# Gathering expert rows two tiles ahead, and a new order at the start of the expert stage

## The chip, the cores and the metric

The kernel runs on one core of one Trainium2 chip. The metric is the device time of one execution in microseconds (us). A time given for a kernel is the median of several executions; rows and durations come from one profiled execution.

The engines are named as the profile names them: PE (TensorE, matrix products; PEld is its weight load), ACT (ScalarE), DVE (VectorE), POOL (GpSimd), SP (SyncE, which here only issues DMAs).

## The reference

One transformer layer over `x` of 32 x 64 tokens of 256 numbers, all float32: a routed mixture of 8 experts, an attention block, a second attention block with a coherence gate, and an FFN with 4-bit rounding. The change touches the expert stage only:

```
gate   = rms_norm(x) @ wg_W + wg_b + cond @ gg_W + gg_b
topk_w, topk_i = top_k(softmax(gate), 2)            # two experts for each token
h1 = relu(x  @ W1[e] + b1[e])                       # 256 -> 512
h2 = relu(h1 @ W2[e] + b2[e])                       # 512 -> 512
out_e = h2 @ W3[e] + b3[e]                          # 512 -> 256
out = sum over the two chosen experts of topk_w * out_e
```

The kernel computes, for each token, only the two experts that were chosen.

## The kernel before

**Tiles.** The 2048 tokens times two choices are sorted by expert into `SLOT_TILES` = 36 tiles of 128 rows. Tiles 0 to 7 hold the first block of expert 0 to 7 each; tiles 13 to 15 are "mixed" (two experts, 64 rows each); the others belong to one expert that is looked up at run time. For each tile the rows of `x` are fetched by an indirect DMA (a *gather*), turned by PE so that features lie on partitions, and sent through three layers.

**Engines in the expert stage.** Every engine has its own program in a fixed order; semaphores join them. A step `j` on PE is `expert_step(j)` (lines 833 to 845): layer 1 of tile `j+1`, the turn of tile `j+2` (`turn_x`, L745, two transposes), layer 2 of tile `j`, layer 3 of tile `j-1`. The loop starts at `j = -2`, so the first steps are short: the turn of tile 0; then layer 1 of tile 0 and the turn of tile 1; then layer 1 of tile 1, the turn of tile 2 and layer 2 of tile 0.

- POOL issues the gathers (L612) into four buffers `xg0` to `xg3`, in tile order, and between them the gathers of bias rows for the mixed tiles (L623 for `b1`, L630 for `b2`).
- ACT copies a turned tile from PSUM into the one buffer `xg_t` (`copy_x`, L1378) and applies bias and rectifier after layer 1 (`relu1`, L1395, four activations of 128 x 128). `relu1` first reads the expert's number into a register (L1389, a TENSOR_LOAD and two register instructions).
- DVE copies the expert's first and second weight matrix into `w1_now` (L1910) and `w2_now` (L1926), and does the second rectifier (L1951).
- SP loads the experts' weights into `arena`, each expert in two halves of 1024 KB (L543). At most two halves are under way: a half is issued when the same half of the expert before has landed. From expert 3 on the load overwrites the scratch of the routing, so the first half of expert 3 also waits for `arena_free` and for the first two gathers (lines 537 to 541).

Layer 1 of tile `j` on PE waits for three things: `xt_set` (the copy of that tile), `h1t_set` (the rectifier of the tile before, which frees the PSUM bank), and `w1_set` (the weights). The turn of tile `j` waits for its gather and for the copy of the tile before.

**Before the first turn** PE runs `keep_busy(40)` (L735, L676): 40 products of 128 x 128 in bfloat16 whose result nobody reads.

The parts of the program that the change touches, with the line numbers of the profile:

Of the kernel before, what the change touches and what calls it, by code (L numbers as in the profile page):

```python
# [54 lines left out]
SLOT_TILES = FULL + MIXED  # L55
# [15 lines left out]
FI = 0.3 * 0.7  # L71
RMS_EPS, LN_EPS, MOD_EPS = 1e-6, 1e-5, 1e-8
XG = 4
TINY, FP4_MAX = 1e-30, 6.0
ROUND = 1.5 * 2.0 ** 22
NEG = -3.0e38
# [25 lines left out]
def exists(t, n):  # L102

    return not isinstance(t, int) or 0 <= t < n
# [17 lines left out]
def mixed(p):  # L122

    return FIRST_MIXED <= p <= LAST_MIXED


def nth(p):

    return p - FIRST_MIXED if mixed(p) else p if p < FIRST_MIXED else p - MIXED


def slot_tile(p):


    if p < EXP:
        return p
    if p < FIRST_MIXED:
        return HOST + p - EXP
    return FULL + nth(p) if mixed(p) else nth(p) - (FULL - HOST)
# [26 lines left out]
def build(nc, t_in, out):  # L166
    ctx = ExitStack()
    with ctx:
# [37 lines left out]

        xg = [sb(f"xg{n}", [P, HID]) for n in range(XG)]
        xg_t = sb("xg_t", [P, KH, P])
# [215 lines left out]
        field_loaded = sem("field_loaded")  # L424
        x_gathered = [sem(f"x_gathered{n}") for n in range(XG)]
        xt_ps = sem("xt_ps")
# [91 lines left out]
        @block.sync  # L518
        def _(sp):

            sp.dma_start(cols[:, 0:GATE_COLS], t_in["cols"][:, 0:GATE_COLS]).then_inc(cols_loaded, 16)
            for k in range(KH):
                sp.dma_start(x_t[:, k, :], t_in["x_t"][k * P:(k + 1) * P, :]).then_inc(xt_loaded[k], 16)
            for k in range(KH):
                sp.wait_ge(xt_loaded[k], 16)
            sp.dma_start(cols[:, GATE_COLS:col_n], t_in["cols"][:, GATE_COLS:col_n]).then_inc(small_loaded, 16)
            sp.dma_start(rows[:, :], t_in["rows"].to_broadcast([P, row_n])).then_inc(small_loaded, 16)
            sp.dma_start(we2, t_in["we2_t"].rearrange("(k p) n -> p k n", p=P)).then_inc(small_loaded, 16)
            sp.dma_start(w_delta, t_in["ffn_dw"].rearrange("(k p) n -> p k n", p=P)).then_inc(small_loaded, 16)
            sp.dma_start(setup_rows, t_in["setup_rows"].to_broadcast([P, set_n])).then_inc(small_loaded, 16)  # L530


            for e in range(EXP):
                for n in range(2):
                    if e:
                        sp.wait_ge(moe_loaded[n], 16 * e)
                    if e == SETUP_FROM and n == 0:

                        sp.wait_ge(arena_free, 1)
                        for g in range(2):  # L540
                            sp.wait_ge(x_gathered[g], 16)
                    at = n * E_SIZE // 2
                    sp.dma_start(arena[:, e * E_SIZE + at:e * E_SIZE + at + E_SIZE // 2],  # L543
                                 t_in["experts"][e][:, at:at + E_SIZE // 2]).then_inc(moe_loaded[n], 16)
                if e == SETUP_FROM - 1:
                    sp.dma_start(b3[:, :], t_in["b3"].to_broadcast([P, EXP * HID])).then_inc(b3_loaded, 16)
                if e == SETUP_FROM + 1:
                    sp.dma_start(w_raw, t_in["ffn_w"].rearrange("(k p) n -> p k n", p=P)).then_inc(ffn_loaded, 16)
            for half in range(2):
                sp.dma_start(half_rows[half * SEQ:(half + 1) * SEQ, :],  # L550
                             t_in["half_rows"][half:half + 1, :].to_broadcast([SEQ, half_n])).then_inc(half_loaded, 16)
            sp.wait_ge(setup_done, 1)
            sp.wait_ge(fa_stored, 16)
            sp.wait_ge(y_ps, LAST_MIXED + 1)
            for dst, name in ((wq, "wq"), (wk, "wk"), (wv, "wv"), (wo, "wo")):
                sp.dma_start(dst[:, :, :], t_in[name].rearrange("(k p) n -> p k n", p=P)).then_inc(w1_loaded, 16)


            sp.wait_ge(w1_set, SLOT_TILES)
            for dst, name in ((wq2, "wq2"), (wk2, "wk2"), (wv2, "wv2"), (wc1, "wc1"), (wout2, "wout2")):  # L560
                sp.dma_start(dst, t_in[name].rearrange("(k p) n -> p k n", p=P)).then_inc(l2w_loaded, 16)
            sp.dma_start(x_in, t_in["x"][0:P, :]).then_inc(x_tile, 16)
            sp.wait_ge(w2_set, SLOT_TILES)
            sp.dma_start(field_t.rearrange("p t q -> p (t q)"),
                         fa_out.rearrange("(o b) q -> o (b q)", o=1).to_broadcast([P, BATCH * SEQ])).then_inc(field_loaded, 16)
            for t in range(TT + 2):
                if exists(t - 2, TT):
                    sp.wait_ge(fin_set, t - 1)
                    sp.dma_start(out[(t - 2) * P:(t - 1) * P, :], fin[t % 2]).then_inc(stored[t % 2], 16)
                if exists(t + 1, TT):  # L570
                    sp.wait_ge(x1_set, t + 1)
                    sp.dma_start(x_in, t_in["x"][(t + 1) * P:(t + 2) * P, :]).then_inc(x_tile, 16)
            for n in range(2):
                sp.wait_ge(stored[n], 16 * TT // 2)
# [3 lines left out]
        def _(pool):  # L578
# [28 lines left out]


            for j in range(SLOT_TILES):
                if j >= XG:  # L610
                    pool.wait_ge(xt_ps, j - XG + 1)
                pool.indirect_dma_start(  # L612
                    out=xg[j % XG][:, :], out_offset=None, in_=t_in["x"],
                    in_offset=bass.IndirectOffsetOnAxis(ap=slot_tok[:, slot_tile(j):slot_tile(j) + 1], axis=0)).then_inc(x_gathered[j % XG], 16)
                if mixed(j - 2):
                    n = nth(j - 2)
                    if n == 0:
                        pool.wait_ge(row_expert_set, 1)
                        pool.wait_ge(setup_done, 1)
                        pool.wait_ge(fa_stored, 16)  # L620
                    if n >= BIAS_BUFS:
                        pool.wait_ge(h1r_set, n - BIAS_BUFS + 1)
                    pool.indirect_dma_start(  # L623
                        out=b1_rows[n % BIAS_BUFS], out_offset=None, in_=t_in["b1"],
                        in_offset=bass.IndirectOffsetOnAxis(ap=row_expert[:, n:n + 1], axis=0)).then_inc(b1_gathered[n % BIAS_BUFS], 16)
                if mixed(j - 4):
                    n = nth(j - 4)
                    if n >= BIAS_BUFS:
                        pool.wait_ge(h2r_set, n - BIAS_BUFS + 1)
                    pool.indirect_dma_start(  # L630
                        out=b2_rows[n % BIAS_BUFS], out_offset=None, in_=t_in["b2"],
                        in_offset=bass.IndirectOffsetOnAxis(ap=row_expert[:, n:n + 1], axis=0)).then_inc(b2_gathered[n % BIAS_BUFS], 16)
# [36 lines left out]
        def _(pe):  # L669
# [3 lines left out]
            def keep_busy(n):  # L673

                for _ in range(n):
                    mm(bank(6, P), ones[:, :], ones[:, :], start=True, stop=True)  # L676
# [55 lines left out]
            for k in range(KH):  # L732
                last = mm(ps[0:BATCH, 7, 0:HID], f_hid[:, k, :], we2[:, k, :], start=k == 0, stop=k == KH - 1)
            last.then_inc(fp_ps, 1)
            keep_busy(40)  # L735

            pe.wait_ge(experts_set, 1)
            flat = arena[:, :]
# [603 lines left out]
        def _(act):  # L1342
# [31 lines left out]
            def copy_x(j):  # L1374
                act.wait_ge(xt_ps, j + 1)
                if j:
                    act.wait_ge(l1_ps, j)
                act.copy(xg_t[:, :, :], ps[:, 5, 0:KH * P].rearrange("p (k q) -> p k q", k=KH)).then_inc(xt_set, 1)  # L1378
# [48 lines left out]
            def expert_step(j):  # L1427
                if mixed(j - 1):
                    take_w3(j - 1)
                    if exists(j + 2, SLOT_TILES):  # L1430
                        copy_x(j + 2)
                    relu2_mixed(j - 1)
                    store_y(j - 2)
                    if exists(j + 1, SLOT_TILES):
                        relu1(j + 1)
                else:
                    if exists(j + 1, SLOT_TILES) and not mixed(j + 1):
                        relu1(j + 1)
                    if exists(j + 2, SLOT_TILES):
                        copy_x(j + 2)  # L1440
                    if j == 0:
                        relu2_first()
                    if mixed(j + 1):
                        relu1(j + 1)
                if exists(j - 1, SLOT_TILES) and not mixed(j):
                    store_y(j - 1)
# [12 lines left out]
            for j in range(-2, LAST - 1):  # L1459
                expert_step(j)  # L1460
                side_stage(j)
# [986 lines left out]
```

## Time and profile before

| | |
|---|---|
| median of 3 runs | 742.73 us (741.77 to 743.66) |
| profiled execution, its own time | 744.68 us |
| its span, first to last instruction | 743.2 us |
| mean granted TensorE clock | 0.986 of full |
| busy: PE, DVE, ACT, POOL | 713.3, 486.3, 287.8, 90.9 us |
| chain that ended last, by engine | PE 94%, DVE 3%, ACT 1%, issue 1% |

The profile lists instructions by start and duration, with the idle time of the engine before them and what ended it. The chain is found by going back from the last instruction, at each step to what released it. Starts are recorded, the ends of products are modelled. The expert stage lies between about 33 and 300 us of the span; the change acts on its first 15 us and on the order of the gathers throughout it.

### The profile page before, as it was taken

The page shows a single profiled execution, that of the slowest core. Times are in us where ns is not written, and L with a number is a line of the kernel's source. Part 1 is how long each engine was busy: PE and PEld are TensorE (multiplying, and loading weights), DVE is VectorE, ACT ScalarE, POOL GpSimd, SP SyncE. Part 2 cuts the span into 40 slices and gives each one's busy share as a digit, 9 for nine tenths or more (in the row PEclk, how much of TensorE's full clock was granted, in tenths as well). Part 3 has the DMA queues.
Part 4 walks back from the last instruction along what each step waited for, and adds up shares of the span by engine and source line. Part 5 has one row for each costly group of instructions (what it writes and reads, how often), then busy time and mean ns, then how long its engine had stood idle before and what let it go on. Part 6 is the DMA issues. An engine that isn't in the chain of part 4 may idle for free.

```text
span 743.2 us, 20463 instructions
## 1 busy us (share of the span) xinstructions
PE 713.3 (96%) x8266; PEld 615.5 (83%) x8266; DVE 486.3 (65%) x1036; ACT 287.8 (39%) x839; POOL 90.9 (12%) x102
## 2 busy tenths in 40 slices
PE   6389999999999999999999999999999999999997
PEld 4279999559999999978778878978888897888785
DVE  4756565743545444334777787787778778777867
ACT  3032121142121221253465446445544654564552
POOL 2121112411111101031101101110110111000000
PEclk9599999999999999999999999999999999999999
DMA  7998111217111102310001000000110010000000
GB/s 262 336 353 322 37 37 56 81 43 257 50 37 37 37 30 69 118 50 23 16 9 30 30 7 25 30 23 10 30 31 9 23 30 24 8 16 16 9 9 23
DMA packets 21402, 49.13 MB, mean 66 GB/s; under 512 B 3323, under 2 KB 14971, under 8 KB 18749
## 3 DMA queue, kind: packets, MB, share of 16 engines
q1 hardware_dynamic: 12256, 32.47, 12.2%
q0 software_dynamic: 3744, 10.49, 4.7%
q10 hardware_dynamic: 5309, 4.87, 2.0%
q8 instruction: 66, 1.08, 0.6%
q14 instruction: 27, 0.22, 0.1%
HBM read 41.00 MB, written 6.82 MB: 64 GB/s over the span
## 4 chain that ended last, share of the span: by engine, by line
PE 94%; DVE 3%; ACT 1%; issue 1%; another core or an unknown queue 0%; DVEq 0%; POOL 0%; ACTq 0%; POOLq 0%
PE ps L897 16%; PE ps L796 15%; PE ps L766 8%; PE ps L923 8%; PE ps L830 7%; PE ps L982 7%; PE ps L948 4%; PE ps L998 3%; PE ps L941 2%; PE ps L973 2%; PE ps L1013 2%; PE ps L1075 2%; PE ps L1032 2%; PE ps L790 1%; PE ps L676 1%; PE ps L1045 1%
## 5 line engine op out<-in xcount | busy, mean ns | idle before, releaser
L897 PE MATMUL ps<-arena,l_weights 128*128 128x128 f32 x1024 | 125.9, 277 | 0.5 <-ACT arena L1470 0.5
L796 PE MATMUL ps<-h_t,w_now 128*128 128x128 f32 x1056 | 123.4, 275 | 1.2 <-DVE h_t L1951 1.2
L796 PEld LDWEIGHTS ps<-h_t,w_now 128*128 128x128 f32 x1056 | 120.5, 192 | 1.4 <-issue 1.4
L897 PEld LDWEIGHTS ps<-arena,l_weights 128*128 128x128 f32 x1024 | 119.3, 192 | 2.3 <-ACT arena L1470 1.0
L1395 ACT ACTIVATE h_t<-ps,cols 128x128 f32<-128x128 f32 x132 | 37.8, 367 | 163.9 <-PE ps L766 149.5
L1926 DVE COPY w_now<-arena 128x2048 f32 x33 | 40.5, 1227 | 83.2 <-PE ps L796 74.7
L1476 ACT ACTIVATE arena<-ps,cols 128x128 f32<-128x128 f32 x256 | 73.9, 387 | 48.0 <-PE ps L897 48.0
L645 POOL DMA_INDIRECT arena<-expert_out,slot_of x32 | 33.1, 1033 | 323.0 <-DVE arena L1979 272.8
L766 PEld LDWEIGHTS ps<-xg_t,w_now 128*128 128x128 f32 x528 | 63.4, 192 | 6.0 <-ACT xg_t L1378 3.5
L766 PE MATMUL ps<-xg_t,w_now 128*128 128x128 f32 x528 | 65.0, 276 | 3.0 <-ACT xg_t L1378 3.0
L612 POOL DMA_INDIRECT xg<-in_x,slot_tok x36 | 41.6, 1155 | 186.4 <-PE ps L745 157.4
L830 PE MATMUL ps<-arena,h_t 128*128 x264 | 62.5, 380 | 0.0
L923 PE MATMUL ps<-l_weights,arena 128*64 128x512 f32 x256 | 61.8, 605 | 0.0
L830 PEld LDWEIGHTS ps<-arena,h_t 128*128 128x128 f32 x264 | 47.7, 191 | 5.1
L982 PE MATMUL ps<-l_weights,arena 128*128 128x256 f32 x224 | 51.5, 383 | 0.0
L982 PEld LDWEIGHTS ps<-l_weights,arena 128*128 128x128 f32 x224 | 41.5, 190 | 5.2
L1910 DVE COPY w_now<-arena 128x1024 f32 x33 | 22.9, 694 | 29.3 <-PE ps L766 20.7
L1951 DVE TENSOR_SCALAR h_t<-ps,cols 128x128 f32<-128x128 f32 x128 | 35.8, 342 | 4.6 <-PE ps L796 4.5
L948 PE MATMUL ps<-ident,arena 128*128 128x128 f32 x256 | 38.3, 273 | 0.1
L2097 DVE TENSOR_TENSOR arena<-ps,half_rows 128x512 f32<-128x512 f32 x32 | 21.9, 686 | 22.7 <-PE ps L973 17.2
L923 PEld LDWEIGHTS ps<-l_weights,arena 128*64 128x64 f32 x256 | 15.6, 136 | 22.5 <-issue 21.4
L1559 ACT ACTIVATE arena<-arena 128x512 f32<-128x512 f32 x32 | 20.2, 631 | 31.6 <-DVE arena L2180 31.6
(366 smaller groups left out, 1097.1 us busy)
## 6 DMA issues: line engine op xcount, KB each, us to landing
arena<-in_experts SPq DMA_DIRECT2D x16, 1024.0 KB
expert_out<-y ACTq DMA_DIRECT2D x36, 128.0 KB
arena<-in_x_t SPq DMA_DIRECT2D x2, 1024.0 KB, 6.2
arena<-in_x SPq DMA_DIRECT2D x16, 128.0 KB
out<-arena SPq DMA_DIRECT2D x16, 128.0 KB, 1.7
b<-in_b SPq DMA_DIRECT2D x1, 1024.0 KB
l_weights<-in_wq SPq DMA_DIRECT2D x1, 1024.0 KB
l_weights<-in_wk SPq DMA_DIRECT2D x1, 1024.0 KB
```

The lines of the kernel that those rows point to most:

```text
L612: pool.indirect_dma_start(out=xg[j % XG][:, :], out_offset=None, in_=t_in["x"], in_offset=bass.IndirectOffsetOnAxis(ap=slot_tok[:, slot_ti ...
L766: last = mm(ps[:, 0, m * P:(m + 1) * P], w1_now[:, k, m * P:(m + 1) * P], xg_t[:, k, :], start=k == 0, stop=k == KH - 1)
L796: last = mm(ps[:, 2, m * P:(m + 1) * P], w2_now[:, k, m * P:(m + 1) * P], h1_t[j % 2][:, k, :], start=k == 0, stop=k == KM - 1)
L830: last = mm(bank(4, HID), h2_t[j % 2][:, k, :], flat[:, bass.ds(at + k * HID, HID)], start=k == 0, stop=k == KM - 1)
L897: last = mm(ps[:, b, c * P:(c + 1) * P], wt[:, k, f:f + P], m_t[:, k, :], start=k == 0, stop=k == KH - 1)
L923: last = mm(ps[r * SEQ:(r + 1) * SEQ, value_bank(t, s), :], m_t[:, k, s * SEQ:(s + 1) * SEQ], wv[:, k, r * 512:(r + 1) * 512], start=k == ...
L948: last = pe.transpose(bank_[:, m * P:(m + 1) * P], p[:, h:h + 2, :], ident[:, :])
L982: last = mm(bank(1, HID), ctx_t[:, c, :], wo[:, c, :], start=c == 0, stop=c == C1 - 1)
L1395: last = f(h1_t[j % 2][:, k, :], ps[:, 0, k * P:(k + 1) * P], ACT.Relu, bias=cols[:, bass.ds(e * KM + at + k, 1)])
L1476: last = f(dst[:, cc, :], ps[:, project_bank(t, n), c * P:(c + 1) * P], ACT.Tanh, bias=col(bias)[:, cc:cc + 1])
L1926: dve.tensor_copy(w2_now[:, :, :].rearrange("p k n -> p (k n)"), arena[:, bass.ds(at, KM * MID)]).then_inc(w2_set, 1)
L1951: last = ts(h2_t[j % 2][:, k, :], ps[:, 2, k * P:(k + 1) * P], cols[:, bass.ds(e * KM + at + k, 1)], 0.0, ALU.add, ALU.max)
```

## The change

Five edits, no change to what is computed:

1. Gather `j` waits until tile `j - 2` is turned (`AHEAD` = 2) where it waited until tile `j - 4` was turned (`XG` = 4 buffers). The four buffers stay. Only two gathers go out at once at the start.
2. The bias gathers keep their place in the stream counted by turned tiles: `b1` of tile `j` follows the gather of tile `j` and not of tile `j + 2`; `b2` likewise.
3. The first half of expert 3 waits for three gathers and not for two.
4. `keep_busy` before the first turn has 28 products and not 40.
5. In ACT's step `j = -1` the copy of tile 1 comes ahead of the rectifiers of tile 0.

```diff
--- before
+++ after
+AHEAD = 2
...
                         sp.wait_ge(arena_free, 1)
-                        for g in range(2):
+                        for g in range(3):
                             sp.wait_ge(x_gathered[g], 16)
...
             for j in range(SLOT_TILES):
-                if j >= XG:
-                    pool.wait_ge(xt_ps, j - XG + 1)
+                if j >= AHEAD:
+                    pool.wait_ge(xt_ps, j - AHEAD + 1)
                 pool.indirect_dma_start(
...
-                if mixed(j - 2):
-                    n = nth(j - 2)
+                if mixed(j):
+                    n = nth(j)
...
-                if mixed(j - 4):
-                    n = nth(j - 4)
+                if mixed(j - 2):
+                    n = nth(j - 2)
...
-            keep_busy(40)
+            keep_busy(28)
...
                 else:
+                    if j == -1:
+                        copy_x(j + 2)
                     if exists(j + 1, SLOT_TILES) and not mixed(j + 1):
                         relu1(j + 1)
-                    if exists(j + 2, SLOT_TILES):
+                    if exists(j + 2, SLOT_TILES) and j != -1:
                         copy_x(j + 2)
```

On ACT, at the start of the expert stage (line, instruction, output<-input; TENSOR_LOAD and the ISA rows read the expert's number), the order before is:

```order
L1378 COPY xg_t<-ps 128x256 [waits xt_ps,experts_set]
L1389 TENSOR_LOAD tile_expert
L1389 ISA x2
L1395 ISA [waits l1_ps]
L1395 ACTIVATE h1_t0<-ps,cols 128x128
L1395 ISA
L1395 ACTIVATE h1_t0<-ps,cols 128x128
L1395 ISA
L1395 ACTIVATE h1_t0<-ps,cols 128x128
L1395 ISA
L1395 ACTIVATE h1_t0<-ps,cols 128x128
L1378 COPY xg_t<-ps 128x256 [waits l1_ps,xt_ps]
```

The same place on ACT with the change (lines after the edit are one to three higher):

```order
L1379 COPY xg_t<-ps 128x256 [waits xt_ps,experts_set]
L1379 COPY xg_t<-ps 128x256 [waits l1_ps,xt_ps]
L1390 TENSOR_LOAD tile_expert
L1390 ISA x2
L1396 ISA [waits l1_ps]
L1396 ACTIVATE h1_t0<-ps,cols 128x128
L1396 ISA
L1396 ACTIVATE h1_t0<-ps,cols 128x128
L1396 ISA
L1396 ACTIVATE h1_t0<-ps,cols 128x128
L1396 ISA
L1396 ACTIVATE h1_t0<-ps,cols 128x128
```

The second copy now stands ahead of the register load and of all four rectifiers.

On POOL, the first gathers of the expert stage, before:

```order
L612 DMA xg0<-in_x,slot_tok 128x256 [waits ids_set]
L612 DMA xg1<-in_x,slot_tok 128x256
L612 DMA xg2<-in_x,slot_tok 128x256
L612 DMA xg3<-in_x,slot_tok 128x256
L612 DMA xg0<-in_x,slot_tok 128x256 [waits xt_ps]
L612 DMA xg1<-in_x,slot_tok 128x256 [waits xt_ps]
```

and with the change:

```order
L613 DMA xg0<-in_x,slot_tok 128x256 [waits ids_set]
L613 DMA xg1<-in_x,slot_tok 128x256
L613 DMA xg2<-in_x,slot_tok 128x256 [waits xt_ps]
L613 DMA xg3<-in_x,slot_tok 128x256 [waits xt_ps]
L613 DMA xg0<-in_x,slot_tok 128x256 [waits xt_ps]
L613 DMA xg1<-in_x,slot_tok 128x256 [waits xt_ps]
```

The third and fourth gather now wait for a turn; from there on the n-th wait of the queue is for the same turn as before, and carries a tile two places later.

## Rows read from the trace of the kernel before

**Rows 1.** The page: granted clock in 40 slices; the last chain by engine.

```profile
PEclk9599999999999999999999999999999999999999
...
PE 94%; DVE 3%; ACT 1%; issue 1%; another core or an unknown queue 0%; DVEq 0%; POOL 0%; ACTq 0%; POOLq 0%
```

**Rows 2.** The chain of waits, 33 to 45 us: start us, us, what.

```profile
33.80 3.24 PE ps L676 x40
37.04 1.38 PE ps L745 x2
38.46 0.04 issue
38.50 0.38 ACT xg_t L1378
...
42.27 0.27 ACT xg_t L1378
42.54 0.04 issue
42.58 2.05 PE ps L766 x16
```

**Rows 3.** Timeline of PE: start, duration, line, operation, count, [idle before <-releaser].

```profile
38.93 2.05 PE L766 MATMUL ps<-xg_t,w_now 128*128 128x128 f32 x16 [1.66 <-ACT xg_t L1378]
40.81 0.38 PE L745 MATMUL ps<-ident,xg 128*128 128x128 f32 x2
...
44.47 0.38 PE L745 MATMUL ps<-ident,xg 128*128 128x128 f32 x2
```

**Rows 4.** Keep-busy products by stretch: length, PE, PEld, clock, DMA share, GB/s.

```profile
34.00:35.00 1.00, 1.00 (x13) 1.00 (x11) 0.50 0.98 418
35.00:36.00 1.00, 1.00 (x15) 1.00 (x14) 0.67 0.80 311
36.00:37.00 1.00, 1.00 (x19) 0.86 (x16) 1.00 0.31 102
```

**Rows 5.** Timeline of POOL, the first gathers.

```profile
32.55 1.10 POOL L612 DMA_INDIRECT xg<-in_x,slot_tok  x1 [27.13 <-DVE slot_tok L1865]
...
35.20 1.04 POOL L612 DMA_INDIRECT xg<-in_x,slot_tok  x1 [0.30 <-issue]
...
38.68 0.94 POOL L612 DMA_INDIRECT xg<-in_x,slot_tok  x1 [1.19 <-PE ps L745]
41.47 2.04 POOL L612 DMA_INDIRECT xg<-in_x,slot_tok  x1 [1.85 <-PE ps L745]
```

**Rows 6.** Timeline of ACT, 41 to 47 us.

```profile
41.13 1.14 ACT L1395 ACTIVATE h_t<-ps,cols 128x128 f32<-128x128 f32 x4 [2.25 <-PE ps L766]
...
45.81 0.20 ACT L1451 ACTIVATE l_weights<-l_weights 32x1 f32<-32x1 f32 x1 [1.98 <-DVE l_weights L2008]
46.48 1.14 ACT L1395 ACTIVATE h_t<-ps,cols 128x128 f32<-128x128 f32 x4 [0.47 <-issue]
```

**Rows 7.** All 36 gathers of rows: time from issue to landing.

```profile
DMA to landing us min/median/max: 2.7/3.3/6.2
```

**Rows 8.** Timeline of SP's queue: the first halves of experts 3, 4 and 6.

```profile
37.10 0.33 SPq L543 DMA_DIRECT2D arena<-in_experts  x1
...
42.42 0.33 SPq L543 DMA_DIRECT2D arena<-in_experts  x1
...
56.15 0.33 SPq L543 DMA_DIRECT2D arena<-in_experts  x1
```

**Rows 9.** Timeline of DVE: the first weight matrix of tiles 3 and 5.

```profile
52.48 0.69 DVE L1910 COPY w_now<-arena 128x1024 f32 x1 [0.44 <-issue]
...
66.04 0.69 DVE L1910 COPY w_now<-arena 128x1024 f32 x1 [0.81 <-PE ps L766]
```

**Rows 10.** Timelines of POOL and PE around the first mixed tile.

```profile
125.19 0.94 POOL L623 DMA_INDIRECT l_weights<-in_b,row_expert  x1 [13.69 <-issue]
126.43 0.94 POOL L612 DMA_INDIRECT xg<-in_x,slot_tok  x1 [0.30 <-issue]
...
131.99 0.44 PE L745 MATMUL ps<-ident,xg 128*128 128x128 f32 x2
```

## The prediction

> **What bounds the kernel now.** I read the page first: PE carries 94% of the chain that ended last, and its clock is granted in full except around the second of the 40 slices, about 18.6 to 37.2 us [rows 1]. PE is therefore the bound, and an edit pays only where it lets PE start sooner or makes it wait. Then the chain of waits from the end of the routing to the first stretch in which PE no longer waits [rows 2]: the reader is to see keep-busy products, the turn of tile 0, ACT's copy, layer 1 of tile 0, ACT again, and at 42.58 layer 1 of tile 1. From there the chain stays on PE without a gap for several tiles. So the start of layer 1 of tile 1 is the place where most of this change is won or lost; a shift there moves everything behind it by the same amount. Last I read, engine by engine, who feeds that place and how much room each feeder has.
>
> **The change part by part.** I count from the start of layer 1 of tile 0, 38.93 [rows 3]; layer 1 of tile 1 begins 3.65 later.
>
> *Shorter keep-busy (edit 4).* The 40 products fill 33.80 to 37.04 [rows 2]. The clock is 0.50 until two thirds of the slice from 35 to 36 are over (mean 0.67), so it rises at about 35.66 [rows 4]: 1.86 us at the lower level, 1.38 at the upper. With d for a product at the upper level and 2d at the lower, 1.86/2d + 1.38/d = 40, so d = 0.058. The twelve that go are the last, at the upper level: 12 x 0.058 = 0.69 us. The turn of tile 0 can then begin at 36.35. Its gather was issued at 32.55 [rows 5]; at the usual 2.7 to 3.3 us to landing [rows 7] it is there by 35.9, an estimate. I take -0.69. Bounds: 0, if the gather arrives only when the turn began before (the slowest gather took 6.2); and -1.39, twelve at the lower level's 0.116.
>
> *Copy ahead of the rectifiers (edit 5).* Layer 1 of tile 1 waits for both, so the later one counts. Before, the rectifiers start at 41.13, 2.20 after my zero and 0.15 after layer 1 has ended (38.93 + 2.05) [rows 3, 6]; the copy follows and ends at 3.61. Now the copy must wait for the turn of tile 1, whose products end at 40.81 + 0.38 = 41.19, or 2.26 [rows 3]; with the same 0.15 it starts at 2.41. Behind it stands the register load that before was done while ACT waited. Its price shows where ACT had just one short activation ahead of it: that began at 45.81, the rectifiers at 46.48, 0.67 later, with the idle time put down to issue [rows 6]. So the rectifiers start at 2.41 + 0.67 = 3.08 and end 1.14 later at 4.22; with 0.04 of issue [rows 2] layer 1 of tile 1 starts at 4.26 and not 3.65. I take +0.61. Bounds: if the load hides under the copy's 0.38 wholly, 2.79 + 1.14 + 0.04 = 3.97, or +0.32; if it starts only when the copy has ended, 2.79 + 0.67 + 1.18 = 4.64, or +0.99. A gain is excluded: the rectifiers can't start before the copy, the copy not before a turn that ends after layer 1.
>
> The Trainium skill ("DMA: Bandwidth & Descriptors", Latency and other measured facts) puts the floor of such a load at about 600 ns. By that page the edit would cost 0.54, and the sum would be 0.07 lower; the measured 0.67 includes the dispatch, and decides.
>
> *Two gathers in front instead of four (edit 1).* Gather 2 goes from 35.20 to where gather 4 stood, behind the turn of tile 0: 38.68 less 0.69 = 37.99 [rows 5]. Landed by 41.3 at 3.3 us, at worst by 44.2. It is needed by the turn of tile 2 at 44.47 - 0.08 = 44.39 [rows 3]. Cost 0; layer 1 of tiles 0 and 1 hides it. From the third gather on each one stands where a gather two tiles later stood, and has two steps of PE; gather 3, at 41.47 - 0.69 [rows 5], is needed one layer 2 (twice layer 1's 2.05) and one layer 1 behind 44.47, so near 50.6: room for 9 us against a worst 6.2.
>
> *Experts behind the third gather (edit 3).* The first half of expert 3 moves from 37.10 [rows 8] to 41.3, by 4.2, and the whole stream behind it on SP's queue with it. That half had landed when SP issued the next at 42.42, and DVE reads it at 52.48; for tile 5 the half has landed at 56.15 and is read at 66.04 [rows 8, 9]. Room 10.1 and 9.9, less 4.2 leaves 5.7 at least. Cost 0, and still 0 with a gather of 6.2 (then the stream is 7.1 later).
>
> *Bias gathers (edit 2).* The `b1` gather of the first mixed tile holds POOL until 125.19; the gather behind it, issued at 126.43, was for tile 16 and is now for tile 14 [rows 10]. Tile 14 is turned at 131.99; at 3.3 us it is there at 129.7. Cost 0, hidden by layers of tiles 11 to 13; at the worst 6.2 us PE waits 0.6 once.
>
> **Sum.** -0.69 + 0.61 = -0.08 us. The profiled execution took 744.68, 1.48 more than its span of 743.2 for what lies around it, so the changed one would take 744.60. That execution is 1.95 above the median of the runs; from the median, 742.65.
>
> **The rivals.**
>
> A, *the first turn ends sooner still.* Its two transposes should take 0.38, yet the chain has 1.38 for it before ACT starts at 38.50 [rows 2, 3]: about 1.0 unexplained. Either gathers 2 and 3, under way just then, hold it up; then edit 1 removes it and the time is 741.65. Or the keep-busy products really end later than recorded, as if all had run at the lower level (33.80 + 40 x 0.116 is 38.44); then twelve fewer save 1.39 and the time is 741.95. Against the first: the turn of tile 1 had gather 4 under way, and POOL, which waited for it, went on 0.28 after its recorded end (41.19 to 41.47).
>
> B, *the clock comes too late* (the other side). The clock rose in this execution 1.86 us into keep-busy. If in another it rises later, the shorter keep-busy is over first, and layer 1 of tile 0, and then of tile 1, run at 0.50: 2.05 more each [rows 3], 744.7 or 746.75. It decides when the clock is still 0.50 as layer 1 of tile 1 begins. For it: keep-busy is what PE did before the rise. Against it: at the rise 24 products were left, of which 12 go, and the waits of 1.66 and about 1.4 us behind did not bring the clock down.
> The Trainium skill ("TensorE: Matmul & The Clock Gate", Part 1) says that the low clock is the default, that activity lifts it, and that the moment differs from run to run. By that rule some executions would be those of B; one trace can't show it, and 12 spare products speak for few.
>
> C, *a gather comes late*, of tile 14 or tile 2, at its worst 6.2 us: +0.2 to +0.6, up to 743.3. The bias gather in front and the experts' loads speak for it, 2.3 us and more of room against.
>
> **How the numbers follow.** The sum as worked out 0.55, A 0.27, B 0.11, C 0.05; 0.02 for something else. 0.3% is 2.2 us, about what a measurement can tell here. The sum, A and C all lie within it, and so does B with one layer: same 0.88. B with two layers, and the rest of the doubt, slower 0.08; faster would need twice A's gain, 0.04. The range goes below to A less 0.75, most of the half spread of the runs (741.77 to 743.66): 740.9. Above, to keep-busy's bound of 0 and the copy's of +0.99 (743.7) and 0.6 for the spread: 744.3.
>
> **What would show it.** In the changed profile: keep-busy 0.6 to 0.7 shorter and the turn of tile 0 as much sooner; layer 1 of tile 1 about 4.26 behind that of tile 0, with ACT's copy ahead of the rectifiers and a gap of about 0.3 between; gather 2 issued near 38 and expert 3 near 41; no wait of PE for a gather at tiles 2, 3 and 14; DVE's copies of first weights not waiting for the experts. ACT's first copy less than 0.5 behind the turn's end would be A, a clock of 0.50 in layer 1 would be B. The prediction is wrong if layer 1 of tile 1 starts more than a microsecond from 42.5, or if a gap opens in PE behind it.

## The result and the profile after

The changed kernel takes 745.16 us (median of 20 executions, 743.29 to 747.06) against 743.15 for the kernel before on the same chip (20 executions): ratio 1.0029, 95% interval 1.0021 to 1.0036, some 2 us slower. The forecast was 742.65, no change, with 744.3 as its upper end. Its profiled execution took 745.81 (span 744.3).

The page after, granted clock and chain by engine [rows 1]:

```profile
PEclk9589999999999999999999999999999999999999
...
PE 94%; DVE 3%; ACT 1%; DMA 1%; issue 0%; POOL 0%; ACTq 0%; DVEq 0%; POOLq 0%
```

PE still carries the chain. The clock of the third slice (37.2 to 55.8 us) goes from 9 to 8 tenths, but a slice of 18.6 us does not show where. The chain of waits of the changed kernel (start us, us, what), for [rows 2]:

```profile
33.53 4.53 DMA xg<-in_x,slot_tok
38.06 0.14 issue
38.19 0.42 PE ps L746 x2
...
38.69 0.38 ACT xg_t L1379
39.07 0.04 issue
39.12 2.05 PE ps L767 x16
41.17 0.23 PE ps L746 x2
41.40 0.02 issue
41.42 0.37 ACT xg_t L1379
```

The reader is to see that the first turn now waits for its gather, not for keep-busy products, and that ACT's copy of tile 1 follows the turn at once. PE's timeline, for [rows 3], goes on from there:

```profile
39.12 2.05 PE L767 MATMUL ps<-xg_t,w_now 128*128 128x128 f32 x16 [0.52 <-ACT xg_t L1379]
41.01 0.38 PE L746 MATMUL ps<-ident,xg 128*128 128x128 f32 x2
43.57 2.84 PE L767 MATMUL ps<-xg_t,w_now 128*128 128x128 f32 x16 [2.18 <-ACT h_t L1396]
46.20 0.63 PE L746 MATMUL ps<-ident,xg 128*128 128x128 f32 x2
46.63 4.39 PE L797 MATMUL ps<-h_t,w_now 128*128 128x128 f32 x32
50.85 1.39 PE L767 MATMUL ps<-xg_t,w_now 128*128 128x128 f32 x11
```

(The last line is short, x11, because the view ends at 52 us.) Layer 1 of tile 1 has waited 2.18 us instead of 1.38, and it then takes 2.84 where that of tile 0 took 2.05. The granted clock by stretch says why (length, PE, clock, DMA share, GB/s):

```profile
43.00:44.00 1.00, 0.43 (x4) 1.00 0.78 205
44.00:45.00 1.00, 1.00 (x10) 0.78 0.94 385
45.00:46.00 1.00, 1.00 (x7) 0.50 0.99 418
46.00:47.00 1.00, 1.00 (x6) 0.50 0.94 393
47.00:48.00 1.00, 1.00 (x7) 0.51 1.09 451
48.00:49.00 1.00, 1.00 (x11) 1.00 1.08 410
```

The clock falls to 0.50 (1.2 GHz) at about 44.56 (mean 0.78 over that microsecond), one microsecond after PE had begun to work again, and comes back at about 47.98. The same place in the kernel before, with PE's timeline below it, has no such stretch:

```profile
45.00:46.00 1.00, 1.00 (x11) 1.00 0.98 401
```

```profile
42.58 2.05 PE L766 MATMUL ps<-xg_t,w_now 128*128 128x128 f32 x16 [1.38 <-ACT xg_t L1378]
...
48.26 1.95 PE L766 MATMUL ps<-xg_t,w_now 128*128 128x128 f32 x16
```

From layer 1 of tile 1 to layer 1 of tile 2 it is 48.26 - 42.58 = 5.68 us before and 50.85 - 43.57 = 7.28 after: **1.60 us lost to the clock**.

Where the rest of the difference between these two executions comes from: the first gather was issued at 33.53 and not at 32.55 [rows 5], in a stage that no edit touches: 0.98. From there to layer 1 of tile 1 it is 10.04 after and 10.03 before. So at layer 1 of tile 2 the changed kernel is 2.59 late: 0.98 + 0.01 + 1.60. That holds until the turn of tile 14, behind which the profiled execution of before had a stall of its own (DVE's and PE's timelines of before):

```profile
131.30 1.23 DVE L1926 COPY w_now<-arena 128x2048 f32 x1 [3.41 <-remote]
```

```profile
133.66 3.81 PE L796 MATMUL ps<-h_t,w_now 128*128 128x128 f32 x32 [1.23 <-DVE h_t L1951]
```

That wait of PE is in none of the 13 other profiles of this study, three of which have gathers four ahead as before; it is not the change. Without it the two executions would lie further apart than 745.81 and 744.68 do: one pair of profiles is not the comparison, the medians are.

### The profile page after: what moved, and what is told of

Its sections match the earlier page's. It is cut to its first block, busy times and chain, and to the rows that moved or that the text cites. A ratio compares the mean times of both kernels' runs of the same rounds, so it can differ in the third digit from the quotient of the medians.

```text
span 744.3 us, 20439 instructions
## 1 busy us (share of the span) xinstructions
PE 715.7 (96%) x8254; PEld 617.8 (83%) x8254; DVE 486.6 (65%) x1036; ACT 288.3 (39%) x839; POOL 93.0 (12%) x102
## 4 chain that ended last, share of the span: by engine, by line
PE 94%; DVE 3%; ACT 1%; DMA 1%; issue 0%; POOL 0%; ACTq 0%; DVEq 0%; POOLq 0%
PE ps L797 16%; PE ps L898 16%; PE ps L767 8%; PE ps L924 8%; PE ps L831 8%; PE ps L983 7%; PE ps L949 4%; PE ps L999 3%; PE ps L942 2%; PE ps L974 2%; PE ps L1014 2%; PE ps L1076 2%; PE ps L1033 2%; PE ps L791 1%; PE ps L746 1%; PE ps L1046 1%
## 5 line engine op out<-in xcount | busy, mean ns | idle before, releaser
L613 POOL DMA_INDIRECT xg<-in_x,slot_tok x36 | 43.7, 1213 | 202.7 <-PE ps L746 173.4
```

The costliest lines, as they stand in the source:

```text
L613: pool.indirect_dma_start(out=xg[j % XG][:, :], out_offset=None, in_=t_in["x"], in_offset=bass.IndirectOffsetOnAxis(ap=slot_tok[:, slot_ti ...
```

## The experiments

Three theories stood against each other. *Clock*: the longer wait before layer 1 of tile 1 brings PE's clock down. *Late data*: a gather or an expert's load comes late. *Plain order*: only the copy's delay counts. Each ratio is to the kernel before on the same chip, with its 95% interval in brackets; it is not simply the quotient of the two medians.

**One edit undone.** The first run is the changed kernel with the rectifiers first again.

```diff
-                    if j == -1:
-                        copy_x(j + 2)
                     if exists(j + 1, SLOT_TILES) and not mixed(j + 1):
                         relu1(j + 1)
-                    if exists(j + 2, SLOT_TILES) and j != -1:
+                    if exists(j + 2, SLOT_TILES):
```

> The changed kernel with its edit 5 undone: the rectifiers of tile 0 come first again on ACT. Clock theory: the changed kernel loses because PE waits 2.2 us between the turn of tile 1 and layer 1 of tile 1, the clock then falls to 0.50, and three to four us of products run at half rate, about 1.6 us. With the rectifiers first the wait is back at about 1.4 us, the clock holds, and keep-busy's 0.7 us stay gained: 0 to 1 us faster than the kernel before. Late-data theory (the third gather and the experts' stream come later and cost somewhere): still about 2 us slower than before. Plain-order theory (the copy's 0.8 us lie on the path and the clock is chance): about 1.2 us slower than before.

Measured: 742.75 (741.83 to 747.38, 12 executions), ratio 1.0003 [0.9989, 1.0016]. Layer 1 of tile 1 waits 1.39 us and runs at full speed (PE's timeline):

```profile
42.37 2.05 PE L767 MATMUL ps<-xg_t,w_now 128*128 128x128 f32 x16 [1.39 <-ACT xg_t L1379]
```

The loss goes with edit 5. The second run keeps edit 5 and undoes edit 4.

```diff
-            keep_busy(28)
+            keep_busy(40)
```

> The changed kernel with its edit 4 undone: 40 keep-busy products again. Clock theory, if the long wait before layer 1 of tile 1 is what brings the clock down: the wait is still 2.2 us, so it stays 1 to 2.5 us slower than before. Clock theory, if the missing keep-busy products are what matters: within 1 us of before, the copy's 0.8 us left. Late-data theory: about 2 us slower.

Measured: 744.62 (5 executions), ratio 1.0034 [1.0021, 1.0047]. The loss stays, and so does its picture:

```profile
42.27 3.52 PE L767 MATMUL ps<-xg_t,w_now 128*128 128x128 f32 x16 [2.18 <-ACT h_t L1396]
...
49.55 1.95 PE L767 MATMUL ps<-xg_t,w_now 128*128 128x128 f32 x16
```

```profile
43.00:44.00 1.00, 1.00 (x7) 0.50 0.94 393
44.00:45.00 1.00, 1.00 (x7) 0.50 1.03 426
```

From layer 1 to layer 1 it is 7.28 again. The number of products in front is not what brings the clock down here.

**One edit alone.** The kernel before with edits 1 to 3 (gathers two ahead, bias gathers, expert 3 behind the third gather):

```diff
+AHEAD = 2
-                        for g in range(2):
+                        for g in range(3):
-                if j >= XG:
-                    pool.wait_ge(xt_ps, j - XG + 1)
+                if j >= AHEAD:
+                    pool.wait_ge(xt_ps, j - AHEAD + 1)
...
```

> The kernel before with edits 1 to 3 alone: gathers two tiles ahead, bias gathers with them, expert 3 behind the third gather; 40 keep-busy products and the rectifiers first as before. Clock theory: no wait of PE changes, within 0.5 us of before. Late-data theory: all of the loss is here, 2 us slower.

Measured: 742.15, ratio 0.9994 [0.9985, 1.0002]. The moved transfers cost nothing, so late data is out. The chain in its profile also has a short first turn, 0.24 where [rows 2] have 1.38:

```profile
36.77 0.24 PE ps L746 x2
```

The kernel before with edit 5 alone:

```diff
+                    if j == -1:
+                        copy_x(j + 2)
...
-                    if exists(j + 2, SLOT_TILES):
+                    if exists(j + 2, SLOT_TILES) and j != -1:
```

> The kernel before with the copy of tile 1 ahead of the rectifiers of tile 0 as its only change (40 keep-busy products, four gathers in front). Clock theory: layer 1 of tile 1 starts some 4.45 behind layer 1 of tile 0 instead of 3.65, TensorE waits about 2.2 us there instead of 1.4, its clock falls to 0.50 in that place and the next 3.4 us are slow as in the changed kernel (+1.6): +0.8 + 1.6 = +2.4 us in executions where it falls, so about 744.6 to 745.5, ratio 1.002 to 1.0033. Plain-order theory: only the +0.8 of the order, clock stays at 1.00 behind its rise, ratio 1.001. Late-data theory: nothing is moved in the gathers or experts, so no more than +0.8 either.

Measured: 745.55, ratio 1.0032 [1.0021, 1.0043], the whole loss, from ACT's order alone. PE's timeline (cut off at 52 us) and clock:

```profile
39.52 2.05 PE L766 MATMUL ps<-xg_t,w_now 128*128 128x128 f32 x16 [0.52 <-ACT xg_t L1378]
41.41 0.38 PE L745 MATMUL ps<-ident,xg 128*128 128x128 f32 x2
43.97 2.94 PE L766 MATMUL ps<-xg_t,w_now 128*128 128x128 f32 x16 [2.18 <-ACT h_t L1395]
...
51.25 0.94 PE L766 MATMUL ps<-xg_t,w_now 128*128 128x128 f32 x7
```

```profile
45.00:46.00 1.00, 1.00 (x6) 0.50 0.98 393
```

43.97 - 39.52 = 4.45 against 3.65 is +0.80, and 51.25 - 43.97 = 7.28 against 5.68 is +1.60: 2.40 us, where the ratio gives 0.0032 x 743.09 = 2.4. The chain of this run, with four gathers in front, has 0.24 for the first turn too:

```profile
38.78 0.24 PE ps L745 x2
```

The kernel before with edit 4 alone:

```diff
-            keep_busy(40)
+            keep_busy(28)
```

> The kernel before with 28 keep-busy products for 40 as its only change. Clock theory with one fall only (the wait of layer 1 of tile 1): that wait keeps its 1.4 us, the clock stays, and the time is 0 to 0.7 us less: ratio 0.999 to 1.000. Clock theory with a late rise as well (the products are over before the clock comes): some executions 2 to 4 us above the rest, the median up to +1, and in a slow execution the clock of 0.50 stands in layer 1 of tile 0 and perhaps of tile 1. If none is more than 1.5 us above 743, the late rise is not what spread the times of the filled kernel.

Measured: 743.19, ratio 1.0001 [0.9991, 1.0011], 741.47 to 744.80 in 11 executions. The clock holds in the profiled one (741.47), but the 0.69 us of the working does not appear in the median (it would be 0.9991, the very edge of the interval). Two executions (744.69 and 744.80) lie just above the 1.5 us over 743 that the expectation named; no profile shows one of them, so this run left the late rise open.

**The wait filled.** If the wait is the cause, products put into it must bring the time back with ACT's new order unchanged. In the step that turns tile 1 PE gets 28 more products behind the turn:

```diff
                     turn_x(j + 2)
+                if j == -1:
+                    keep_busy(28)
```

> The changed kernel with 28 more keep-busy products on PE between the turn of tile 1 and layer 1 of tile 1, where PE waits 2.2 us; they need about 1.6 us at full clock and delay nothing. Clock theory: PE is busy in the wait, the clock holds through layers 1 and 2, and some 1.6 us come back: within 0.7 us of before. Late-data and plain-order theories: no change, 2 us slower than before.

Measured: 743.63, ratio 1.0022 [1.0008, 1.0036], but in two groups: 742.17 to 744.20 in 7 executions, 745.83 to 746.81 in 4. The profiled one (742.17) is as the clock theory says:

```profile
39.20 1.73 PE L677 MATMUL ps<-ones 128*128 128x128 bf16 x28
41.55 2.02 PE L767 MATMUL ps<-xg_t,w_now 128*128 128x128 f32 x16 [0.61 <-issue]
```

In the upper group the mean granted clock of an execution is 0.982 to 0.984, in each of the other seven 0.985, so the clock has a part in it; no profile shows where. The same filling with 40 products in front of the first turn:

```diff
-            keep_busy(28)
+            keep_busy(40)
...
+                if j == -1:
+                    keep_busy(28)
```

> The changed kernel with 40 keep-busy products, and 28 more on TensorE between the turn of tile 1 and layer 1 of tile 1 (they fill most of its wait of 2.2 us). Clock theory: the clock stays at 1.00 in layer 1 of tile 1 and the 1.6 us that the kernel with 40 products and no filling lost come back: some 742.6 to 743.2 against 744.6, ratio about 1.000, and without the upper group of 744 to 747 that the filling behind 28 products had. Plain-order theory: filling a wait changes nothing, ratio stays at 1.0034. If the upper group stands here too, the number of products before the first turn is not its cause.

Measured: 743.30, ratio 1.0009 [0.9999, 1.0018], 742.70 to 744.45: no upper group. In PE's timeline layer 1 of tile 1 comes 43.30 - 38.85 = 4.45 behind that of tile 0, as late as in the changed kernel, and the clock stays up:

```profile
38.85 2.05 PE L767 MATMUL ps<-xg_t,w_now 128*128 128x128 f32 x16 [0.52 <-ACT xg_t L1381]
...
43.30 2.02 PE L767 MATMUL ps<-xg_t,w_now 128*128 128x128 f32 x16 [0.62 <-issue]
...
48.95 1.95 PE L767 MATMUL ps<-xg_t,w_now 128*128 128x128 f32 x16
```

48.95 - 43.30 = 5.65. In the run with 40 products and no filling that stretch took 7.28: products that compute nothing give back 1.63 us in these profiles, and some 1.4 (medians) to 1.9 us (ratios) in the times. What is left, 0.0009, fits the order alone (+0.80 us would be 0.0011), though the interval of this run also holds no loss at all.

**The upper group.** With 28 products in front and 20 in the wait:

```diff
-                    keep_busy(28)
+                    keep_busy(20)
```

> The changed kernel (28 keep-busy products) with 20 products in the wait before layer 1 of tile 1, where 28 of them gave times in a lower group near 742.2 and an upper one near 746.5. Late-rise theory: the upper group stands here too (its cause is in front of layer 1 of tile 0): median 742.3 to 745, some executions above 745.5, and a profile that falls among them shows 0.50 in layer 1 of tile 0. Filling-too-long theory (28 products at the lower clock outlast the wait): with 20 the upper group comes down to 745 or less.

Measured: 743.70, ratio 1.0007 [0.9994, 1.0019]; 741.76 to 746.19. That refutes the filling that is too long: the upper group has not come down to 745. The profiled execution took 745.51 and shows how one execution comes to be so slow. Chain, timeline of PE, clock:

```profile
32.89 5.13 DMA xg<-in_x,slot_tok
```

```profile
34.07 2.81 PE L677 MATMUL ps<-ones 128*128 128x128 bf16 x28
38.15 0.41 PE L746 MATMUL ps<-ident,xg 128*128 128x128 f32 x2 [1.27 <-DMA xg<-in_x,slot_tok]
39.07 3.17 PE L767 MATMUL ps<-xg_t,w_now 128*128 128x128 f32 x16 [0.52 <-ACT xg_t L1381]
```

```profile
36.00:37.00 1.00, 0.88 (x12) 0.82 0.41 143
...
38.00:39.00 1.00, 0.41 (x2) 1.00 0.00 0
39.00:40.00 1.00, 0.93 (x7) 0.89 0.00 0
40.00:41.00 1.00, 1.00 (x7) 0.50 0.37 119
```

Gather 0 took 5.13 us this time. The 28 products were over at 36.88, PE waited 1.27 and then 0.52, and its clock, up since about 36.4, fell at 39.78 in layer 1 of tile 0, which took 3.17 and not 2.05. This is no late rise, as I had expected, but the same fall, behind two waits with only the turn between them. The three slowest executions of this run have a mean granted clock of 0.983, the other nine 0.985 or 0.986; that each of the slow ones had a late gather is not shown.

Next, far fewer products, on the kernel before:

```diff
-            keep_busy(40)
+            keep_busy(16)
```

> The kernel before with 16 keep-busy products for 40 as its only change (so few that they are over before the clock has come). In the profiles so far the clock rose 1.7 to 3.1 us behind the first product, and 16 products at the lower level take 16 x 0.116 = 1.86 us. Late-rise theory: the turn of tile 0 and layer 1 of tile 0 run at 0.50 (layer 1 up to 4.1 us instead of 2.05) in most executions, the 1.4 us saved in front are paid back and more: 743.5 to 745.5, ratio 1.0005 to 1.003. Plain-order theory: fewer products let the turn begin earlier, down to the landing of gather 0 (2.9 to 4.5 us behind its issue): 1 to 1.5 us less, 741.6 to 742.1, ratio 0.998 to 0.9987, clock of 1.00 in layer 1 of tile 0.

Measured: 743.37, ratio 1.0014 [0.9995, 1.0033], 740.63 to 747.76. Neither theory was right on every execution: some are 2 us below the kernel before, 5 of 12 above 745.5. The profiled one (742.50) had its gather after 3.29 us, a wait of 0.41 and a clock that held in layer 1. I have no profile of one above 745.5; the mean granted clock of those five is 0.979 to 0.984, of the other seven 0.983 to 0.987, so a lower clock is likely there too.

Two attempts at a better kernel: edits 1 to 3, rectifiers first, a small filling, with 34 and with 40 products in front.

```diff
-            keep_busy(40)
+            keep_busy(34)
...
+                if j == -1:
+                    keep_busy(12)
```

> The kernel before with the gathers two tiles ahead and the experts' load behind the third (as the run of these edits alone), 34 keep-busy products for 40, and 12 products in the wait before layer 1 of tile 1 (1.4 us there, rectifiers first). Clock theory: the clock is up and stays, six products less save 0.35 us, and the first turn keeps its 0.24: 741.8, ratio 0.9990 (0.998 to 0.9995). If late rises matter already at 34, some executions lie 2 us above and the ratio is 1.000 or more. Plain-order theory: 0.35 us less too, so this run is for a better kernel and for the late rise, not for the fall.

Measured: 742.75, ratio 1.0001 [0.9989, 1.0013], with 746.31 among 12 executions.

```diff
-            keep_busy(34)
+            keep_busy(40)
```

> The kernel before with edits 1 to 3 (gathers two ahead, bias gathers, expert 3 behind the third gather), all 40 keep-busy products, rectifiers first, and 12 products in the wait of 1.4 us before layer 1 of tile 1. Clock theory: with 40 products a late gather 0 opens no long wait in front of the first turn, with the filling none stands in front of layer 1 of tile 1 either: no upper group above 745.5 as with 34 products, the times as in the run of edits 1 to 3 alone, 741.6 to 743.7, ratio 0.9985 to 1.0002. If the upper group stands here with 40 products, a late gather is not its cause. Late-data theory: the gathers' order alone gives or takes more than 0.3%, in either direction.

Measured: 743.15, ratio 1.0001 [0.9990, 1.0012], 742.07 to 743.94, no upper group. Executions above 745.5, in the kernels whose layer 1 of tile 1 does not wait 2.18 us: 5 of 12 with 16 products, 7 of 46 with 28 (four kernels), 1 of 12 with 34, 0 of 34 with 40 (three kernels). The kernel before has 40 products too, and 4 of its 120 executions lie above 745.5. So they become rarer with more products in front, but 40 do not exclude them; what causes them in the kernel before no profile shows. No version beats the kernel before by more than the runs can tell; edits 1 to 3 alone come closest.

Last, the changed kernel once more, for a second profile:

> The changed kernel once more, for a second profile. Clock theory: layer 1 of tile 1 again at 0.50 (2.8 to 3.5 us) behind a wait of 2.2 us. Chance theory (the fall in the one profile was an accident): layer 1 of tile 1 at 1.00, 2.05 us, and a time near 743.5.

Measured: 744.55, and the fall is there again:

```profile
42.28 2.66 PE L767 MATMUL ps<-xg_t,w_now 128*128 128x128 f32 x16 [2.18 <-ACT h_t L1396]
...
49.57 1.95 PE L767 MATMUL ps<-xg_t,w_now 128*128 128x128 f32 x16
```

49.57 - 42.28 = 7.29. In all four profiles with the wait of 2.18 unfilled the clock falls, at a cost of 1.60 or 1.61 us.

## Why the prediction was wrong

**Shorter keep-busy, -0.69: not in the result.** The arithmetic of d = 0.058 was fair, but the products cover a transfer whose time I took as 2.7 to 3.3. Gather 0 took 2.9 in three profiles, 4.53 in the changed kernel's (the turn then waited for it, 38.06) and 5.13 in another. Where it is late less is saved, or the clock falls; alone the edit gave 1.0001. In the changed kernel's profile the 28 products themselves took nearly as long as the 40 before (3.24 in [rows 2]); PE's timeline and the granted clock:

```profile
34.71 3.17 PE L677 MATMUL ps<-ones 128*128 128x128 bf16 x28
```

```profile
37.00:38.00 1.00, 0.88 (x9) 0.63 0.19 74
```

The clock rose only at 37.74, 3.03 us behind the first product and not 1.86. In the run of edit 4 alone the median is nearer to the bound of 0 than to -0.69, and there is a loss beyond that bound that I excluded.

**Copy ahead of the rectifiers, +0.61: mis-sized within its bounds.** It measured 4.45 - 3.65 = +0.80. ACT's timeline of the changed kernel:

```profile
41.42 0.37 ACT L1379 COPY xg_t<-ps 128x256 f32<-128x256 f32 x1 [2.36 <-PE ps L746]
42.32 1.14 ACT L1396 ACTIVATE h_t<-ps,cols 128x128 f32<-128x128 f32 x4 [0.53 <-issue]
```

From the copy's start to the rectifiers it is 0.90, not the 0.67 of [rows 6]: 0.53 of the register load stands in the open behind a copy of 0.37, where 0.47 stood behind an activation of 0.20, so the longer instruction in front hid no more of it.

**Edits 1 to 3, 0: right.** Ratio 0.9994 [0.9985, 1.0002] alone. Gather 2 was issued at 38.87, 0.88 later than I had it, and PE waited for none of the moved gathers. DVE's idle times that the profile of the changed kernel puts down to an expert's load (0.71 and 0.26 us) are as long at the same places before, where they are put down to issue.

**The step that failed** stands under rival B: "the waits of 1.66 and about 1.4 us behind did not bring the clock down". From that I priced the new wait by its own length alone, in the sum and in every rival. My own term had made it longer, 1.38 + 0.61 (it became 2.18), and the waits of [rows 3] said nothing about one of that length behind the turn of tile 1. The 1.66 itself belongs to the one execution whose first turn ended late; in all 13 other profiles that wait is 0.52. B had the right resource and the right layer at a wrong moment: it let the clock rise late, in some executions and because of edit 4; the clock rose in time and fell again, in each profile with the wait of 2.18 unfilled, because of edit 5. With edit 4 one profile shows a fall without that wait, the one with the gather of 5.13. The sum by what the runs showed is +0.80 + 1.60, less at most 0.69: 1.7 to 2.4, against a measured 0.0029 x 743.15 = 2.2 (1.6 to 2.7). Another 0.4 of the distance from 742.65 to 745.16 lies in the starting point: I counted from the median of three runs, 742.73, and 20 gave 743.15.

The Trainium skill ("TensorE: Matmul & The Clock Gate", Part 1) has the clock return to its low level when the engine has been idle. The traces agree that idle time brings it down: it fell behind the wait of 2.18 us and held behind that of 1.38. The place is worth seeing: in the changed kernel the low clock shows 1 us after PE had started again (0.25 to 1.2 us in the four profiles), so that the wait looks innocent and the work behind it slow.

**Rival A.** The excess of 1.0 us in the first turn does go away, but not by edit 1: the run of edit 5 alone has four gathers in front and 0.24 as well. What held the turn in that one execution stays open. A gather 0 that landed late does not explain it: SP's load of expert 3, which waits for gathers 0 and 1, went out at 37.10 [rows 8], so both had landed by then, and the turn, which takes 0.2 to 0.4 us, ended at 38.42 [rows 2].

**Rival C** did not come: the moved gathers of tiles 2 and 14 made PE wait in no profile, although the slowest gather of the changed kernel took 8.4 us, and not the 6.2 that I had as the worst.

## What to carry to other kernels

A wait on TensorE has two prices: its own length, and the half-speed work behind it once it is long enough to bring the clock down. Before lengthening one, or thinning the work between two of them, find in the trace the longest after which the granted clock held, and treat anything beyond it as unpriced, not as linear. A single length is no safe limit: waits of 1.27 and 0.52 us with only a turn between them brought the clock down in one profile here, while 1.38 alone did not in any. Products that compute nothing, put into such a wait, show which of the two prices was paid.

## What was not expected of the hardware

The fall is regular: in layer 1 of tile 1, behind 1.38 or 1.39 us of waiting, the clock held in five of five profiles; behind 2.18 us it fell in four of four, and the stretch to the next layer 1 took 7.28 or 7.29 us instead of 5.68 each time. In all four the low clock began after PE had gone back to work. And the same gather, at the same place, took 2.9 to 5.13 us to land from one execution to the next.
